# A gated delta-rule layer in fp32: the next head group's weights loaded in four pieces and a remainder over five turns

## The reference

```python
def attn(x):                                   # x: layer-normed input
    q, k, v, z = split((x @ w_qkvz.T), per head)      # 32 heads, 64 wide each
    q, k, v = causal_conv4(q, k, v)                   # 4 taps, per channel
    g = -exp(A_log) * softplus(a + dt_bias); beta = sigmoid(b)    # b, a from x @ w_ba.T
    q = l2norm(q) * 64 ** -0.5;  k = l2norm(k)
    for t in range(256):                              # state S: 64 x 64 per head
        S = S * exp(g[t])
        S = S + outer(k[t], (v[t] - k[t] @ S) * beta[t])
        o[t] = q[t] @ S
    o = o * rsqrt(mean(o * o) + eps) * norm_weight * sigmoid(z)
    return o @ w_out.T
x = x + layernorm(attn(layernorm(x)))
x = x + layernorm(ffn(layernorm(x)))           # silu-gated, 256 -> 1024 -> 256
```

## Time and profile before

| | |
|---|---|
| runs | 3074.32, 3086.29, 3082.26 us; median 3082.26 |
| profiled execution | 3074.76 us |
| its span | 3073.0 us |
| PE busy | 2933.7 us, 95% |
| DVE busy | 2452.5 us, 80% |
| ACT busy | 1865.0 us, 61% |
| GpSimd (POOL) busy | 1442.5 us, 47% |
| moved by DMA | 241.88 MB, mean 79 GB/s |

### The profile page before, as it was taken

The page is one execution under the profiler, slowest core; times in us unless marked ns, Lnnn a source line. Parts: engine busy times, 40 slices in busy tenths (PEclk is TensorE's granted clock), DMA queues, the critical chain, the costliest instruction groups (busy, mean ns, idle before and its releaser), DMA issues. The chain is left out here.

```text
span 3073.0 us, 101762 instructions
## 1 busy us (share of the span) xinstructions
PE 2933.7 (95%) x42816; PEld 1943.6 (63%) x42816; DVE 2452.5 (80%) x5418; ACT 1865.0 (61%) x3434; POOL 1442.5 (47%) x1096
## 2 busy tenths in 40 slices
PE   6799999999999999999999999999999999789998
PEld 3366666666666666666666666666666666655555
DVE  7588888888888888888888888888888888746564
ACT  6466666666665666666666666666666666424332
POOL 1555555555555555555555555555555555200000
PEclk9899999999999999999999999999999999989999
DMA  5344444444444444444444444444444444300000
GB/s 155 81 82 99 78 77 85 85 98 80 84 84 90 79 77 83 98 83 81 85 98 79 83 83 96 81 79 81 85 98 82 84 82 82 83 21 23 26 14 21
DMA packets 806582, 241.88 MB, mean 79 GB/s; under 512 B 723952, under 2 KB 744816, under 8 KB 804976
## 3 DMA queue, kind: packets, MB, share of 16 engines
q1 hardware_dynamic: 806128, 235.36, 39.0%
HBM read 120.13 MB, written 39.58 MB: 52 GB/s over the span
## 5 line engine op out<-in xcount | busy, mean ns | idle before, releaser
L1370 PE MATMUL bank<-xT,w_sb 128*128 128x512 f32 x2048 | 1025.6, 625 | 26.8 <-DVE kq L1115 15.7
L796 POOL TENSOR_TENSOR kq<-kq,product 128x510 f32<-128x510 f32 (+2 forms) x384 | 478.3, 1253 | 765.7 <-ACT product L895 755.8
L1370 PEld LDWEIGHTS bank<-xT,w_sb 128*128 128x128 f32 x2048 | 359.6, 192 | 346.3 <-issue 291.9
L895 ACT ACTIVATE product<-bank,cw 128x512 f32<-128x512 f32 x576 | 381.9, 690 | 2.9 <-POOL kq L796 1.2
L956 ACT COPY delta<-bank 128x256 f32<-128x256 f32 x256 | 94.9, 371 | 418.5 <-PE bank L1438 417.0
L1115 DVE SCALAR_TENSOR_TENSOR kq<-bank,cw,kq 128x510 f32<-128x510 f32 (+2 forms) x384 | 286.2, 745 | 57.3 <-ACT kq L889 48.1
L784 POOL TENSOR_TENSOR dec_ap<-gcrow,gcb 128x1024 f32<-128x1024 f32 x64 | 134.0, 2093 | 278.3 <-DMA gcb<-gcb_d 278.3
L1142 DVE TENSOR_TENSOR x_un<-x_un,prod_un 128x15 f32<-128x15 f32 (+7 forms) x960 | 236.0, 246 | 33.0
L1381 PE MATMUL bank<-kq 64*64 64x128 f32 x4096 | 260.1, 270 | 2.4 <-POOL kq L796 2.0
L1485 PE MATMUL bank<-wo,u_sq 128*128 128x256 f32 x1024 | 257.6, 395 | 2.8 <-DVE u_sq L1208 2.8
L1463 PEld LDWEIGHTS bank<-ap_mat,delta 64*64 64x64 f32 x4096 | 219.4, 136 | 48.0 <-issue 48.0
(11 more groups left out here) (169 smaller groups left out, 5758.5 us busy)
## 6 DMA issues: line engine op xcount, KB each, us to landing
xT<-xT_d SPq DMA_DIRECT2D x64, 512.0 KB, 3.7
gcrow<-gcrow_d SPq DMA_DIRECT2D x128, 256.0 KB, 4.5
k_r<-k_tok SPq DMA_DIRECT2D x512, 64.0 KB, 2.0
v_r<-k_tok SPq DMA_DIRECT2D x512, 64.0 KB, 2.0
a_d<-ap_mat SPq DMA_DIRECT2D x256, 64.0 KB, 2.0
z_t<-z_d SPq DMA_DIRECT2D x256, 64.0 KB, 2.5
w_sb<-in_w_qkvz SPq DMA_DIRECT2D x8, 1024.0 KB, 5.8
x_un<-eye_un SPq DMA_DIRECT2D x64, 128.0 KB, 4.2
```

The source lines that it names most:

```text
L796: nc.gpsimd.tensor_tensor(t[:, :, d:SEQ], t[:, :, d:SEQ], prod[:, :, 0:SEQ - d], ALU.add).then_inc(tap_added[i], 1)
L895: ins = nc.scalar.activation(products[i % 4], bank[:, :], ACT.Identity, scale=cw_two[m.grp % 2][:, w:w + 1])
L1370: ins = nc.tensor.matmul(bank[:, :], w_two[m.grp % 2][:, h, s * P:(s + 1) * P], xT[:, h, :], start=(h == 0), stop=(h == HT - 1))
```

## The change

`weights` takes the step instead of the group, and is called in every turn of SP, right behind `v_turned` and before the wait for `kx_done`. For the third to the sixth step of a group it issues one quarter of the next group's projection weights, 256 KB of 512 columns, and for the seventh step the convolution and the output weights. `load_x` loads `xT` only. The count that PE waits for follows.

```diff
+        WP = 4
...
-                    def weights(g):
+                    def weights(m):
+                        g, i = m.grp + 1, m.off % NSP - 2
+                        if g == NHG or not 0 <= i <= WP:
+                            return
+                        if i < WP:
+                            c = slice(i * HT * 8 * P // WP, (i + 1) * HT * 8 * P // WP)
+                            sp.dma_start(flat(w_two[g % 2])[:, c], w_qkvz[g][:, c]).then_inc(w_in, 16)
+                            return
                         if g > 1:
                             for k in range(2):
                                 sp.wait_ge(op_full[k], NSP * (g - 1))
-                        sp.dma_start(w_two[g % 2][:, :, :].rearrange("p h t -> p (h t)"), w_qkvz[g]).then_inc(w_in, 16)
                         sp.dma_start(cw_two[g % 2][:, :], conv_w[g]).then_inc(cw_in, 16)
                         sp.dma_start(wo[g % 2][:, :, :].rearrange("p a h -> p (a h)"), w_out[g]).then_inc(wo_in, 16)
...
                     def load_x(m):
...
-                        if m.off % NSP == NSP - 2 and m.grp + 1 < NHG:
-                            weights(m.grp + 1)
...
                             v_turned(s[4])
+                        if s[2]:
+                            weights(s[2])
                         if s[3]:
                             wait_for(sp, kx_done[0], s[3], 1)
...
-                            pe.wait_ge(w_in, 16 * m.grp + 16)
+                            pe.wait_ge(w_in, 16 * WP * m.grp + 16)
```

## The result

| | kernel before | changed kernel |
|---|---|---|
| median of 4 runs | 3080.92 us | 3048.09 us |
| range | 3074.32 to 3086.29 | 3046.81 to 3049.53 |
| profiled execution, span | 3074.76, 3073.0 | 3049.53, 3047.7 |
| DVE busy | 2452.5 | 2487.5 |

The ratio is 0.9903, with an interval of 0.9884 to 0.9922: 1.0% faster, 33 us in the medians, where 40 were forecast. The two profiled executions are 25.2 us apart; that of before lies 0.4 us above its fastest run, that of after is the slowest of its four. So the two profiles differ by less than the medians do. The lines of `kernel.py` after the edit stand 7 further down: L1401 is now L1408, L1428 is L1435, L1165 is L1172, L1154 is L1161.

A forecast was written before the change was run, and what follows sets the result against it. PE bounds ordinary turns at 38.71 us; the seven weights turns' excess of 39.75 us goes and nothing is added: 3074.76 - 39.75 = 3035.0, with 7.5 to the median 3042.5, forecast 3042 us, range 3028 to 3062.

The forecast's parts named there:

- The range and the direction: Whole kernel: 3028 to 3062 us around 3042, 1.3% less; chance of faster 0.86.
- Excess of the seven turns, all removed: Seven weights turns take 310.72 us against 270.97 for ordinary ones; all 39.75 us would go.
- the clock's share: PE's extra busy time at lower clock in the weights turns, 18.7 us, would go with the wait at L1401.
- Why `x_row` was late: Behind the weights, `x_row` is 3.0 us late: 1.51 issuing plus 1.5 slower landing; PE has about 0.5 to spare.
- What it adds, 0: Pieces in 35 turns cost 0 in SP's issuing, DMA engines, k's and v's landing, and PE's order.
- Rival 1: Pieces hold up PE's code loads: new pauses, one per group costing 6 to 27 us, middle 3059; chance 0.16.
- Rivals 2 and 3: 2: L1401's wait isn't the weights', 3082, chance 0.04. 3: pieces delay v at DVE's L1154, 3109, chance 0.06.
- the bound on what ordinary turns do: Ordinary turns last 38.71 us, PE busy throughout; making only a transfer earlier can't shorten them.
- the L1428 waits: PE's small waits on DVE, 8.1 us, some following weights turns; the time could go further down by them.
- the forecast's own sign of being wrong: Wrong altogether if L1401 still waited or the 38.71 us turns became longer everywhere.
- the 7.5 us that I added: Distance of the profiled execution, 3074.76, below the median 3082.26; added to 3035.0 to give 3042.5.

The follow-up runs named there:

- gate_before: Kernel before, with POOL's masking made to wait until DVE's scaling of v has ended: 3048.14 us (0.9886 of the kernel before).
- three_small_issues: Changed kernel with POOL's masking waiting for DVE's scaling of v, convolution weights back behind `xT` as three 4 KB transfers: 3015.01 us (0.9839).
- pieces_behind_xT: Changed kernel with POOL's masking waiting for DVE's scaling of v, the same weight pieces issued behind `xT`, ahead of `x_row`: 3017.47 us (0.984).
- no_weights_race: Changed kernel, no wait added, with the weights of groups 2 to 7 not loaded: 3050.64 us (0.9896).
- gate_after_again: Changed kernel with POOL's masking made to wait for DVE's scaling of v, run on another chip: 3017.76 us (0.9787).
- one_behind_v: Changed kernel with POOL's masking waiting for DVE's scaling of v, projection weights as one 1 MB transfer behind v's: 3020.57 us (0.9793).

## Why the prediction was right or wrong, point by point

- *The range and the direction* held: 3048.09 in 3028 to 3062, 1.0% against 1.3%.
- *Excess of the seven turns, all removed*: right. 39.75 became 2.81, and those 2.81 are the race. That the clock's share would go with the wait: right, the clock stood at 1.00. But 39.75 was the excess of one execution: in gate_before it is 27.3, and the change is worth 25 us there.
- *Why `x_row` was late*: half wrong. The sum 1.51 (issuing) + 1.5 (landing) closed with 0.5 us to spare because the ordinary turn that I compared with was among the tightest: its last `x_row` landed 6.79 us after `xT`, later than in 35 of the 40. In the median it is 6.37, so `x_row` was 3.6 us late and 1.0 was to spare. three_small_issues shows that issuing alone makes 0.6 of these 3.6, which the 1.0 to spare hides, and pieces_behind_xT that there is room for about 256 KB. About 3 us of the lateness come from the bytes.
- *What it adds, 0*: right on every line. SP's gap held the issues (0.58 us each, not 0.36), k was not late, v's landing was not slowed, and no_weights_race has it as a whole: without the transfers nothing is gained. The Trainium skill's preference for transfers of at least 1 MiB (DMA: Bandwidth & Descriptors, "Rules for kernel authors") did not show in the time: four pieces and one whole, behind v, took the same (gate_after_again, one_behind_v).
- *Rival 1*, code loads: the pauses in the small matmuls stayed, 15 and 17, with two new ones at other lines, 2.1 us in sum. Rivals 2 and 3 did not happen: the wait left with the weights, and DVE waited less for v.
- *The step that failed* is the bound on what ordinary turns do. I took 38.71 us as their length, noted the L1428 waits (8.1 us in 20) as something that could only shrink, "some of which follow weights turns", and put them on the low side of the range. They grew to 19.4 us in 42, since two engines start within nanoseconds of each other and compete: of the 40 turns that are neither weights turns nor the first two of a group, 12 had a long scaling before and 30 have one after. So the forecast's own sign of being wrong, longer ordinary turns, came true in part. The sum stayed in its range because the loss, 12.9 us, was smaller than the gain, and the median came within 6 us of 3042 by some luck: the profiled executions are 25.2 us apart, not 39.75, and the 7.5 us that I added for the distance from that of before to its median did not hold for the changed kernel, whose median lies 1.4 us below its profiled execution.
  The trace of before had it to read: an ordinary turn of 39.43 us (664.51 to 703.94) with DVE 35.17 us busy, beside those of 38.71 with 33.1, and a line of DVE with a median of 1220 ns and a maximum of 3426.

## What to carry to other kernels

A large prefetch costs by the bytes that it puts in front of the next transfer that is waited for, far more than by its issue. Either another place or pieces that the slack can take is enough: one whole behind v and four pieces in the old place took 3020.57 and 3017.47 us, and both at once 3017.76 and 3022.91. To tell what is to spare, take all ordinary turns and not one. And where turns come in two lengths, look for one instruction of VectorE with two durations and for the GpSimd instruction that starts with it: a wait that fixes their order brought 60 us here together with the change, and 35 without it. The order matters: fixed the other way round, the changed kernel became 2.3% slower (3122.21 us).

## What was not expected of the hardware

- A DVE instruction of 1.22 us and a POOL instruction of 2.34 us that start within 25 ns of each other take 1.22 and 3.44, or 3.42 and 2.34, and a few nanoseconds decide which. In the changed kernel it fell out the same way up to 17 turns in a row. When POOL has a queue of work, a DVE instruction released between two of its instructions still loses 0.8 us (2.02 for 1.22).
- The time from issue to landing of the last `x_row` behind `xT` was 3.5 us, and 1.9 where it was issued 2.3 us later.
- The same 17 to 18 us of PE's waiting came with 11 us more busy time at a lower clock in one execution and 19 in another, and the granted clock of a turn did not follow the length of its wait (0.92 after 2.03 us, 1.00 after 2.59).
- Deciding the race for DVE is worth as much as the change: it took 1.1% off the kernel before (3048.14 us), the change alone 1.0%, and both together 2.0% and 2.1% (3022.91 and 3017.76 us).
